# Another plan over the 32 slots for TensorE and ScalarE, and z's silu as z/2 (1 + tanh(z/2))

## The reference, cut to what matters

```python
# layer 1: a small state-space layer, per token
y0  = C * scan(decay, dt * B * u)            # 64 channels; then y0 @ Wo + bo
# layer 2: a Mamba block on that output
xn  = (x - mean) * rsqrt(var + 1e-5) * ln_g + ln_b
xz  = xn @ W_in;  x_br, z = split(xz, 2)     # 1024 columns each
xb  = silu(conv4(x_br) + conv_b)
Bm, Cm = xb @ W_b, xb @ W_c                  # 16 states
delta  = softplus(xb @ W_delta + b_delta)
h_t = exp(delta * A) * h_(t-1) + delta * Bm * xb;  y = sum(h_t * Cm) + xb * Dp
out = y * silu(z) @ W_out + residual
# layers 3 and 4: a low-rank mixing matrix from cond, a quantized feed-forward
```

## Time and profile before

| | |
|---|---|
| median of 3 runs | 2785.42 us (2783.49 to 2786.21) |
| profiled execution | 2786.61 us, of which the span of the trace 2784.9 us |
| PE busy | 2361.1 us (85%) |
| DVE busy | 2307.4 us (83%) |
| POOL busy | 1725.0 us (62%) |
| ACT busy | 1702.0 us (61%) |
| granted TensorE clock, mean | 0.928 |

### The profile page before, as it was taken

One profiled execution on the slowest core, in us unless ns is written; L12 is line 12 of the kernel. 1 busy time (PEld: TensorE's weight loads), 2 busy tenths in 40 slices (PEclk: granted clock), 3 DMA queues, 4 the chain that ended last, 5 costly groups with the idle time before them and its releaser, 6 DMA issues. The chain is left out here.

```text
span 2784.9 us, 34215 instructions
## 1 busy us (share of the span) xinstructions
PE 2361.1 (85%) x11488; PEld 1604.4 (58%) x11520; DVE 2307.4 (83%) x2326; ACT 1702.0 (61%) x3314; POOL 1725.0 (62%) x2025
## 2 busy tenths in 40 slices
...
DMA packets 47435, 151.74 MB, mean 54 GB/s; under 512 B 7973, under 2 KB 8869, under 8 KB 44206
## 3 DMA queue, kind: packets, MB, share of 16 engines
...
...
## 5 line engine op out<-in xcount | busy, mean ns | idle before, releaser
L463 POOL TENSOR_TENSOR ring<-ring,Cbc 128x512 f32<-128x512 f32 x1024 | 1287.2, 1278 | 44.2
L851 DVE TENSOR_TENSOR_SCAN ring<-a_ps,ring 128x1024 f32<-128x1024 f32 x512 | 1164.9, 2278 | 85.7 <-ACT a_ps L674 85.7
L674 ACT ACTIVATE a_ps<-delta,nA 128x255 f32<-128x255 f32 x2048 | 851.2, 465 | 371.6 <-DVE ring L851 370.0
L1045 PE MATMUL yT_ps<-ident,ring 128*128 128x128 f32 x4096 | 606.7, 287 | 238.0 <-POOL ring L463 235.5
L1045 PEld LDWEIGHTS yT_ps<-ident,ring 128*128 128x128 f32 x4096 | 473.3, 145 | 371.8 <-POOL ring L463 335.6
L843 DVE TENSOR_TENSOR ring<-u_ps,Bbc 128x1024 f32<-128x1024 f32 x512 | 620.1, 1211 | 73.9 <-PE yT_ps L1045 67.1
L1011 PE MATMUL work<-xb,big 128*128 128x256 f32 x2048 | 465.6, 380 | 0.0
L456 POOL TENSOR_TENSOR carry<-ring,half 128x4 f32<-128x4 f32 x512 | 122.9, 240 | 496.0 <-DVE ring L851 493.3
L1011 PEld LDWEIGHTS work<-xb,big 128*128 128x128 f32 x2048 | 380.8, 191 | 53.7 <-issue 7.4
L1027 PE MATMUL work<-Wout,xb 128*128 128x512 f32 x512 | 252.7, 632 | 0.0
L980 PE MATMUL work<-y0s,big 128*128 128x256 f32 x1024 | 232.2, 379 | 0.0
...
## 6 DMA issues: line engine op xcount, KB each, us to landing
...
```

The lines of the kernel that those rows point to most:

```text
L463: nc.gpsimd.tensor_tensor(hp, hp, Cbc[:, G * g + GP * c:G * g + GP * c + GP, :], ALU.mult)\
L674: r = nc.scalar.activation(a_ps[q % 2][:, i, 1:T], delta[:, par, dt, 1:T], ACT.Exp, scale=nA[:, dt, s:s + 1])
L851: dve.tensor_tensor_scan(ring[:, q % RING, :, :].rearrange("p g t -> p (g t)"), a_ps[q % 2][:, :, :].rearrange("p g t -> p (g t)"), ring[: ...
L1045: r = pe.matmul(yT_ps[:, tt, :], ring[:, q % RING, i, P * tt:P * tt + P], ident[:, :], is_transpose=True, start=False, stop=(g == NG - 1 a ...
```

## The change

1. **z's silu.** The matrix Mz that makes z is halved when it is made (`mz_copy`, scale 0.5), so the Z banks hold z/2. ACT writes tanh(z/2) to zs straight out of PSUM (`ztanh`), one ACTIVATE of 128 x 512 for each of the four jobs. DVE computes (tanh + 1) * (z/2) into zs, with z/2 still in the bank (`zsilu`), and frees the bank with a memset behind it. Tanh is in Exp's table; ACT's copies, its two Silus and their two table loads go.
2. **Variance.** `stats` moves from DVE to ACT: a Square with an accumulated sum over the WO bank, scaled by 1/sqrt(512). It needs centred columns, so the WO jobs use a centred Wo (`Wcen`, made once). DVE's bn_stats, bn_aggr and the addition go; POOL's `rstd` adds epsilon itself.
3. **Order.** All the plans are another one: x(j, m) starts at slot 10 instead of 12 and ends at 15 instead of 16, BC moves from 19 to 17, the silu of x from 18 to 17, Z0 and Z1 from 12 to 19 and 20, Z2 and Z3 from 17 and 20 to 24 and 25, and the 16 parts of delta stand in slots 19 to 31 instead of 20 to 31. YB changes its bank, the Z jobs too.

```diff
-SUMS = (26, 6)
+SUMS = (27, 6)
...
+        Wcen = big[0][:, 5 * DI:5 * DI + D]
...
             def rstd(n):
...
+                nc.gpsimd.tensor_tensor(nrm[:, 1, :], nrm[:, 0, :], half[:, NT + G:2 * NT + G], ALU.add)\
+                    .then_inc(s_rstd, 1)
+                pool.wait_ge(s_rstd, 2 * n + 1)
+                nc.gpsimd.tensor_tensor(nrm[:, 1, :], nrm[:, 1, :], half[:, 0:NT], ALU.pow).then_inc(s_rstd, 1)
...
+                def stats(tt):
+                    job = f"WO{tt}"
+                    ps = take(job)
+                    nc.scalar.activation(ps[:, :], ps[:, :], ACT.Square, scale=float(D) ** -0.5,
+                                         accum_out=nrm[:, 0, tt:tt + 1]).then_inc(free[BANK[job]], 1)
...
-                def zcopy(j):
+                def ztanh(j):
                     ps = take(f"Z{j}")
...
-                    nc.scalar.activation(zs[:, fp, j // 2, 512 * (j % 2):512 * (j % 2) + 512], ps[:, :], ACT.Copy)\
-                        .then_inc(free[BANK[f"Z{j}"]], 1)
+                    nc.scalar.activation(zs[:, fp, j // 2, 512 * (j % 2):512 * (j % 2) + 512], ps[:, :], ACT.Tanh)\
+                        .then_inc(s_tz, 1)
...
-                    for tt in range(NT):
-                        v = zs[:, fp, tt, :]
-                        r = nc.scalar.activation(v, v, ACT.Silu)
-                    r.then_inc(s_zs, 1)
...
+                def zsilu(j):
+                    dve.wait_ge(s_tz, 4 * n + j + 1)
+                    v = zs[:, fp, j // 2, 512 * (j % 2):512 * (j % 2) + 512]
+                    dve.scalar_tensor_tensor(v, v, 1.0, work[BANK[f"Z{j}"]][:, :], ALU.add, ALU.mult).then_inc(s_zs, 1)
+                    dve.wait_ge(s_zs, 4 * n + j + 1)
+                    dve.memset(mark[:, :], 0.0).then_inc(free[BANK[f"Z{j}"]], 1)
...
-                next_plan = {4: [gates0], 5: [scan0], 6: [lambda: stats(0)], 8: [lambda: stats(1), stats_end],
-                             13: [keep_y0]}
+                next_plan = {4: [gates0], 5: [scan0], 13: [keep_y0], 20: [lambda: zsilu(0)], 21: [lambda: zsilu(1)],
+                             25: [lambda: zsilu(2)], 27: [lambda: zsilu(3)]}
...
-                        20: [("n", z, 3), ("n", dl, 0, 0), ("n", dl, 0, 1)], 21: [("n", dl, 0, 2), ("n", dl, 0, 3)],
+                        23: [("n", dl, 1, 1), ("n", dl, 1, 2)], 24: [("n", dl, 1, 3), ("n", z, 2)], 25: [("n", z, 3)],
```

More of the change, by code:

```diff
@@ L42 @@
 NV = 228
-SUMS = (26, 6)
-BANK = {"PRJ": 0, "GT3": 1, "WOUT0": 1, "WO0": 0, "WO1": 0, "WOUT1": 1, "YT": 0, "YB": 1, "GT0": 1,
-        "Z0": 0, "Z1": 1, "XB0": 0, "XB1": 1, "XB2": 0, "XB3": 1, "Z2": 0, "GT1": 1, "BC": 0, "Z3": 1, "DL0": 0,
-        "DL1": 1, "GT2": 1, "DL2": 0, "DL3": 1}
+SUMS = (27, 6)
+BANK = {"PRJ": 0, "GT3": 1, "WOUT0": 1, "WO0": 0, "WO1": 0, "WOUT1": 1, "YT": 0, "YB": 0, "GT0": 1,
+        "XB0": 0, "XB1": 1, "XB2": 0, "XB3": 1, "BC": 0, "GT1": 1, "Z0": 1, "Z1": 1, "DL0": 0,
+        "DL1": 1, "Z2": 0, "Z3": 0, "GT2": 1, "DL2": 0, "DL3": 1}
 BACK = ["GT3", "WOUT0", "WOUT1"]
@@ L102, in scan_phase @@
         ident = sb("ident", [P, P])
-        half = sb("half", [P, NT + G])
+        half = sb("half", [P, 2 * NT + G])
         sc0 = sb("sc0", [P, 8])
@@ L370, in _ @@
                                     base=0, pattern=[[-1, P]], channel_multiplier=1).then_inc(s_ident, 1)
+            nc.gpsimd.memset(half[:, NT + G:2 * NT + G], EPS).then_inc(s_zero, 1)
             ident1 = half[:, NT:NT + G].rearrange("p (g o) -> p g o", o=1)
             def rstd(n):
-                pool.wait_ge(s_stat, 2 * n + 2)
-                nc.gpsimd.tensor_tensor(nrm[:, 1, :], nrm[:, 0, :], half[:, 0:NT], ALU.pow).then_inc(s_rstd, 1)
+                pool.wait_ge(s_zero, 11)
+                pool.wait_ge(free[BANK["WO1"]], jobs_before("WO1", n - 1) + 1)
+                wait(pool, s_rstd, 2 * n)
+                nc.gpsimd.tensor_tensor(nrm[:, 1, :], nrm[:, 0, :], half[:, NT + G:2 * NT + G], ALU.add)\
+                    .then_inc(s_rstd, 1)
+                pool.wait_ge(s_rstd, 2 * n + 1)
+                nc.gpsimd.tensor_tensor(nrm[:, 1, :], nrm[:, 1, :], half[:, 0:NT], ALU.pow).then_inc(s_rstd, 1)
             def first_col(half, n, bp):
@@ L422, in step @@
                         delta_sum(0, k + 1, 1 - par)
-                    if front and q == 8:
+                    if front and q == 7:
                         rstd(k + 1)
@@ L751, in keep_y0 @@
                     dve.tensor_copy(y0k[:, fp, :], y0[:, :]).then_inc(s_c0, 1)
-                def stats(tt):
-                    job = f"WO{tt}"
-                    dve.wait_ge(full[BANK[job]], jobs_before(job, k) + 1)
-                    dve.bn_stats(stat[:, tt, :], work[BANK[job]][:, :]).then_inc(free[BANK[job]], 1)
-                def stats_end():
-                    dve.wait_ge(free[BANK["WO1"]], jobs_before("WO1", k) + 1)
-                    dve.memset(mark[:, :], 0.0)
-                    for tt in range(NT):
-                        r = dve.bn_aggr(mv[:, tt, :], stat[:, tt, :])
-                    r.then_inc(s_stat, 1)
-                    dve.wait_ge(s_stat, 2 * n + 1)
-                    dve.tensor_scalar(nrm[:, 0, :], mv[:, :, 1], EPS, None, ALU.add).then_inc(s_stat, 1)
                 def mx_scale():
@@ L976, in x @@
                 def x(j, m):
+                    if j == 0 and m == 0:
+                        pe.wait_ge(free[BANK["YB"]], jobs_before("YB", k) + 1)
+                        if isinstance(k, int) and k == -1:
+                            pe.wait_ge(s_mxc, ND)
                     ps = work[BANK[f"XB{j}"]] if m else give(f"XB{j}")
```

68 lines of the change are left out of this document (36 added, 32 removed).

## The result

The changed kernel takes 2792.5 us (median of 11 runs, 2788.41 to 2793.48) against 2784.28 (11 runs, 2783.49 to 2786.21): ratio 1.0027, 95% interval 1.0018 to 1.0036. It is slower by 0.3%, where 2770 was forecast. The profiled execution took 2792.67, its span 2790.6.

What follows compares the result with a forecast made beforehand. DVE's chain was taken to bound the scan phase: waits -3.1, work +1.6, so -1.5 us a step; with +0.5 for PE's clock -1.0, times 15 is -15 us, about 2770 us, range 2743 to 2797.

Steps and rivals of the forecast that it cites:

- Step -1: The step without a scan: taken as even, delta parts 3 us longer through bank 0, but DL1 full earlier.
- The waits after: DVE's waits per step in the new plan: 0.25, 1.2, 2.35, 1.05, 3.6, 0.75 and 0.66, together 9.9 against 13.0 us.
- slot 11's 0.25: DVE's wait for a_ps 11, ready at 11.8 and wanted at 11.6 us after scan 7's end.
- DVE's work: Per step: four added products 3.2 us, second statistics gone 1.64, net +1.6 us (+1.0 to +2.2).
- The first statistics: DVE's first bn_stats, 0.59 us, counted as nothing because the u product behind it ends with POOL's sum for delta.
- The base: Step length of the kernel before, 133.56 us, between the column products of slot 23 at 1013.55 and 1147.11.
- The clock allowance: PE's late clock at Z1 (1.3 us) and Z2 (up to 3), one step in four for either: +0.5 us a step.
- the clock: Rival: PE's clock falls ahead of Z2 in most steps, +1.1 us a step, about 2801 us; chance 0.19.
- threshold of 5.1: The clock rival decides once DVE's wait ahead of Z2's product is over 3.6 + 1.5 = 5.1 us.
- Rows 7: Profile rows at 1126.16: PE had 0.30 us of work in 3.34, then the granted clock was 0.50, the 1.2 GHz level.
- no wait for transposes came back in slots 28 to 31: Test of the prediction: new waits for PE's transposes in slots 28 to 31 would show it wrong.
- the waits of 3.6 and 1.05: New DVE waits ahead of the products for Z2 (3.6 us, the largest) and Z1 (1.05 us).

## Why the prediction was wrong, step by step

Forecast -1.0 us a step times 15, 2770; measured +0.07 a step and 2792.5. The mechanism of the waits was right. Two terms of the sum failed, each by 0.44 us a step: the length of the step before, taken from one instance, and the allowance for PE's clock. Step -1 and the last step add to it. By the steps of the prediction:

- **The waits after** were right: 9.32 in the short step against 9.9, each within 0.1 but slot 11's 0.25, which is not there.
- **DVE's work** was forecast at +1.6. The four products take 0.73 each with the memset (2.9, not 3.2). The first statistics were rightly counted as nothing: u grew from 1.89 to 2.49. What was missed is the u product of slot 0, about 1.3 after and 0.84 before in most steps: +0.5. In sum a short step is 132.25, where -1.5 from 133.56 made 132.06: 0.2 off.
- **The base failed.** 133.56 was read from one period. The mean was 133.12, so 0.44 a step, 6 us in 14, was gained on paper only.
- **The clock allowance failed by as much.** It was +0.5, from one late step in four at Z1 and at Z2. The price of one was within its bound (1.69, up to 3). But Z2 is late in six of fifteen, Z1 in none, and a_ps 31, which the allowance did not name, in four. The mean over the short step is 133.19 - 132.25 = 0.94 a step: 0.44 more, 6 us. The run with added matmuls has 0.15 in place of the 0.94, and so has the one with Z1's product in slot 22.
- **Step -1 was not even.** The first scan of block 0 starts at 120.44, before at 118.09: +2.35. In that step Z3 waits for bank 0 behind Z2, DL2 behind Z3, and PE's idle time ahead of DL2 is 3.19 us:

```profile
103.76 1.13 PE L1000 MATMUL work<-big,y0s 128*128 128x512 f32 x2 [1.53 <-DVE mark L774]
108.08 16.08 PE L1019 MATMUL work<-xb,big 128*128 128x256 f32 x64 [3.19 <-DVE mark L774]
```

  With the tanh form undone ACT frees the bank, and the 3.19 is the same, only the 1.53 is 0.69. So DVE's product accounts for 0.8 us of this chain at most. The start itself goes with the variance: it is at 118.2 and 118.9 in the two runs of the new order with the variance on DVE, and at 119.6 to 121.4 in the changed kernel and the eight runs with the variance on ACT that leave POOL's first sum in slot 27. What in that form costs the time is not shown.

- The profiled spans differ by 5.7 us. 2.35 of them are step -1, 1.0 the fourteen periods, and the remaining 2.3 lie behind the silu of x in step 14, where scan 31 waits 2.08 for a_ps (a late clock again) and waited for nothing before. The medians differ by 8.2; the rest is how the profiled runs stand to their medians.

Of the rivals, the clock came nearest. Its mechanism holds (5.18 us, just past its threshold of 5.1), but in six steps, not in most; hence 2792.5 and not 2801. What the prediction takes from the page TensorE: Matmul & The Clock Gate of the Trainium skill, that short idle times make the clock swing, stands in its section "A second HAM failure mode: psum-queue depth-cycling" and not in the one named. Rows 7 show a fall behind 3 us of idle time, not behind short ones; the changed kernel's trace agrees with the sentence in part, with falls behind idle times of 1.2 and 0.6 us in six of fifteen steps at Z2 and in none at Z1. As forecast, no wait for transposes came back in slots 28 to 31 (0.17 in one step apart), and u got no shorter.

Behind the single terms is a question that the prediction did not ask. It walked the waits of 3.6 and 1.05 correctly and took them as given, though each came from the product's slot and not from the work: moving either by one slot gives 31 us, of which some 11 in Z1's case are late clocks that went with it. Nor did it price the parts against one another: the tanh form as placed loses 25 to 33 us, which is more than the 23 that the order brings.

What stays open is why the clock falls ahead of Z2 in just those six steps. Four edits end it: added matmuls in two places, the same in one, Z1's product in slot 22, and POOL's sum in slot 8. The last two leave PE's order alone, and with the sum in slot 8 PE's idle times ahead of Z2 are unchanged as well. That a changed step displaces the fall to another place fits all four, but no run isolates it.
